# Weights transposed at the end of each slot and x1 added a slot earlier, in a cross-attention and FP4 feed-forward kernel

## What is computed

```python
def block(x, context, Wq, Wk, Wv, Wo, bo, w_gate, w_up, w_down):
    n = layernorm(x)
    q, k, v = n @ Wq, context @ Wk, context @ Wv          # 16 heads of 64
    attn = softmax(q k^T * 64**-0.5)                      # per head, 1024 x 154
    x = x + (attn v) @ Wo + bo                            # x1
    n = layernorm(x)
    gate, up = fp4(n) @ fp4(w_gate).T, fp4(n) @ fp4(w_up).T   # 704 hidden
    return x + fp4(silu(gate) * up) @ fp4(w_down).T
```

## Time and profile before

| | us |
|---|---|
| median of 3 runs | 984.53 (983.6 to 984.84) |
| the profiled execution, its own time | 986.75 |
| span of its trace, first to last instruction | 984.9 |
| PE busy | 857.0 (87%) |
| DVE busy | 757.5 (77%) |
| ACT busy | 534.0 (54%) |
| POOL busy | 529.5 (54%) |
| mean granted TensorE clock, share of full | 0.973 |

### The profile page before, as it was taken

One profiled execution on the slowest core, in us unless ns is written; L12 is line 12 of the kernel. 1 busy time (PEld: TensorE's weight loads), 2 busy tenths in 40 slices (PEclk: granted clock), 3 DMA queues, 4 the chain that ended last, 5 costly groups with the idle time before them and its releaser, 6 DMA issues.

```text
span 984.9 us, 21389 instructions
## 1 busy us (share of the span) xinstructions
PE 857.0 (87%) x6254; PEld 812.8 (83%) x6254; DVE 757.5 (77%) x2176; ACT 534.0 (54%) x1879; POOL 529.5 (54%) x677
## 2 busy tenths in 40 slices
PE   4786789999999999989989999989999999999874
PEld 3666789988888998888978888889888888888863
DVE  5857788877778888867878888876877888887762
ACT  4454455556565555556555555556555555655520
POOL 2545666554535656545554656554553656555651
PEclk9888999999999999999999999999999999999986
DMA  7101000001010000001000000001000000000000
GB/s 215 39 11 49 7 17 13 22 13 44 7 33 17 13 23 11 21 14 39 12 28 23 12 22 12 21 8 33 23 7 23 12 18 12 16 11 12 7 11 11
DMA packets 19869, 23.13 MB, mean 23 GB/s; under 512 B 2642, under 2 KB 18234, under 8 KB 19770
## 3 DMA queue, kind: packets, MB, share of 16 engines
q1 hardware_dynamic: 19770, 21.94, 7.2%
HBM read 17.74 MB, written 4.19 MB: 22 GB/s over the span
## 4 chain that ended last, share of the span: by engine, by line
PE 63%; DVE 21%; issue 8%; ACT 4%; POOL 2%; DMA 1%; DVEq 1%; SPq 0%; POOLq 0%; ACTq 0%
PE ps_g L1015 10%; PE ps_q L937 8%; PE ps_s L975 8%; PE ps_t L985 5%; PE ps_o L998 5%; PE ps_o L1000 5%; PE ps_o L999 5%; DVE negmax L782 3%; DVE pT_lo L637 3%; PE ps_m L865 3%; PE ps_g L900 3%; PE ps_m L1025 3%; PE ps_m L1027 2%; PE ps_m L1026 2%; DVE scales L667 2%
## 5 line engine op out<-in xcount | busy, mean ns | idle before, releaser
L472 POOL TENSOR_TENSOR probs<-probs,rsum 128x308 f32<-128x308 f32 x256 | 180.0, 703 | 284.2 <-DVE rsum L746 283.6
L610 ACT ACTIVATE probs<-ps_s,negmax 128x154 f32<-128x154 f32 x512 | 194.7, 386 | 229.4 <-DVE negmax L782 228.2
L998 PE MATMUL ps_o<-B_sb,pT_lo 128*128 128x256 f32 x640 | 183.6, 287 | 38.5 <-DVE x_both L804 33.9
L782 DVE TENSOR_REDUCE negmax<-ps_s 128x2 f32<-128x308 f32 x256 | 121.3, 474 | 78.4 <-PE ps_s L975 76.6
L1000 PE MATMUL ps_o<-B_sb,pT_hi 128*128 128x256 f32 x640 | 181.2, 283 | 0.0
L999 PE MATMUL ps_o<-B_sb,pT_hi 128*128 128x256 f32 x640 | 180.9, 283 | 0.0
L998 PEld LDWEIGHTS ps_o<-B_sb,pT_lo 128*128 128x128 f32 x640 | 121.7, 190 | 45.3 <-issue 42.9
L637 DVE TENSOR_TENSOR pT_lo<-ps_t,pT_hi 128x256 fp32r<-128x256 f32 (+1 forms) x256 | 122.7, 479 | 42.6 <-ACT pT_hi L514 37.4
L985 PE MATMUL ps_t<-ident,probs 128*128 128x128 f32 x640 | 115.0, 278 | 35.9 <-DVE pT_lo L637 35.3
L1015 PE MATMUL ps_g<-WGU,xqT_hi 128*128 128x352 f32 x512 | 136.6, 349 | 3.5 <-DVE B_sb L637 1.9
L514 ACT ACTIVATE pT_hi<-ps_t 128x256 fp32r<-128x256 f32 (+1 forms) x256 | 111.4, 435 | 29.1 <-PE ps_t L985 22.7
(11 more groups left out here) (149 smaller groups left out, 2236.7 us busy)
## 6 DMA issues: line engine op xcount, KB each, us to landing
xa<-in_x_dram SPq DMA_DIRECT2D x33, 128.0 KB, 2.1
xr<-in_x_dram SPq DMA_DIRECT2D x32, 128.0 KB, 2.0
out_dram<-y_xn SPq DMA_DIRECT2D x32, 128.0 KB, 1.7
W_sb<-in_L_xattn_Wk_dram SPq DMA_DIRECT2D x4, 512.0 KB, 4.4
W_sb<-in_L_xattn_Wv_dram SPq DMA_DIRECT2D x3, 512.0 KB, 3.6
probs<-in_L_xattn_Wq_dram SPq DMA_DIRECT2D x1, 1024.0 KB, 7.0
Wo_sb<-in_L_xattn_Wo_dram SPq DMA_DIRECT2D x1, 1024.0 KB, 6.6
VT<-in_ctx_dram SPq DMA_DIRECT2D x1, 384.0 KB
```

The lines of the kernel that those rows point to most:

```text
L472: pool.tensor_tensor(unit, unit, rsum[:, 2 * u:2 * u + 2].unsqueeze(2) .to_broadcast([P, 2, M]), ALU.mult).then_inc(norm_p, 1)
L610: ins = act.activation(probs[:, h, 0:M], ps_s[k % 2][:, s * M:(s + 1) * M], ACT.Exp, bias=negmax[:, h:h + 1], accum_out=sums[:, h:h + 1])
L782: dve.tensor_reduce(negmax[:, 2 * k:2 * k + 2], ps_s[k % 2][:, 0:UM].rearrange("p (h m) -> p h m", h=2), AX_X, ALU.max, negate=True).then_ ...
L998: pe.matmul(ps_o[:, 0:C], lo[:, j, :], w[:, 0:C], start=first, stop=False)
```

## The change

VectorE's add of the residual moves from the middle of its slot 4 to the end of its slot 3, with its waits. ScalarE's copy of x1 to `y`, which must come before it, moves from the end of slot 3 to the end of slot 2. On TensorE the transposes of the weights move from behind `attend` to behind all products of the slot (hidden and x transposes, gate and up, down, q, setup jobs); only the transposes of the raw weights of the start stay behind them.

```diff
@@ scalar: step
-                    if down and k == 3:
+                    if down and k == 2:
                         at = pair - 2 + par
                         act.wait_ge(x1_v, d + 1)
...
                         act.activation(y[1 - par], x1[1 - par], ACT.Copy).then_inc(y_a, 1)
@@ vector: step
                     if before and k == 4:
-                        dve.wait_ge(o_mm, PAIRS * (e + 1))
-                        dve.wait_ge(xr_p, e + 1)
-                        if some(d + 1):
-                            dve.wait_ge(y_a, d + 1)
-                        elif not some(e):
-                            dve.wait_ge(raw_mm, RAW_T[3])
-                        dve.tensor_tensor(x1[1 - par], xr[1 - par][:, :], ps_o[:, 0:C], ALU.add).then_inc(x1_v, 1)
                         if some(e):
                             dve.wait_ge(xln2_a, e)
                         stats(x1[1 - par], st2, mv2, ve2, nm2, (x1_v, e + 1), ln2_v, 5 * e)
...
+                    if before and k == 3:
+                        dve.wait_ge(o_mm, PAIRS * (e + 1))
+                        dve.wait_ge(xr_p, e + 1)
+                        if some(d + 1):
+                            dve.wait_ge(y_a, d + 1)
+                        elif not some(e):
+                            dve.wait_ge(raw_mm, RAW_T[3])
+                        dve.tensor_tensor(x1[1 - par], xr[1 - par][:, :], ps_o[:, 0:C], ALU.add).then_inc(x1_v, 1)
@@ tensor: step
                     if own and k >= 4:
                         attend(t, k - 4, setup if kind in ("start", "roll") else None)
-                    if before and k < 2:
-                        turn_probs(e, k + PAIRS - 2)
-                    if own and k >= 2:
-                        turn_probs(t, k - 2)
...
                     for job in jobs_at(setup, k):
                         make(job, setup[1])
+                    if before and k < 2:
+                        turn_probs(e, k + PAIRS - 2)
+                    if own and k >= 2:
+                        turn_probs(t, k - 2)
                     if turn_at(t, k, 0) is not None:
                         chunk_transposes(turn_at(t, k, 0))
```

## The result

The changed kernel takes 1008.46 us (median of 4 runs, 1006.26 to 1009.55) against 984.1 of the kernel before on the same chip: a ratio of 1.0244 (1.0225 to 1.0263). It is slower, as forecast, but by 24 us and not by 6, and half a microsecond past the upper end of the range.

The account below looks back on a forecast made before the run. No engine was taken to bound both halves of a tile pair alone: VectorE paced even slots 5 to 7, then TensorE. Terms of +6.9, +0.9, some -1 and a tail of nothing, about +6 on 984.5, gave 990 us, range 966 to 1,008.

Parts of the forecast that it names:

- The maximum of slot 5: VectorE, even tiles: starts 4.93 us after S, the start of slot 4's first score product, against 5.21 before.
- even to odd: From slot 4 of an even ordinary tile to slot 4 of the odd one: about +1.1 us, 27.2 against 26.07.
- odd to even: From slot 4 of an odd ordinary tile to slot 4 of the next even one: -0.2 us, 24.85 against 25.05.
- Tiles with setup jobs: Tiles v, k, roll and settle: TensorE paces them; their steps per eight tiles were -1.4, +1.1, -0.8 and +1.6 us.
- the start takes some 1 off: Start of the kernel: about 1 us gained, as what stands behind the waiting transposes waits for the same VectorE.
- into v: Step into the setup tile v: -1.4 us, saved at x1 and slot 7, less 0.7 in slots 1 and 2.
- v to k: Step from setup tile v to setup tile k: +1.1 us, reckoned as even to odd.
- k to roll: Step from setup tile k to roll: -0.8 us, x1's and slot 7's savings against later banks and a longer gate wait.
- roll to settle: Step from setup tile roll to settle: +1.6 us, x1 saves 1.54 but slots 6, 7 and 0 wait for VectorE.
- (A): Rival, whole kernel: faster, VectorE swallows the phase shift; 960 to 975 us, at best 951; chance 0.30.
- (C): Rival, nearly every slot: the hand-over stalls both engines, much slower, about 1,010 to 1,030 us; chance 0.12.
- (D): The forecast itself, whole kernel: slower by 0.2 to 2%, 986.5 to 1,003 us; chance 0.43.

Follow-up runs that it names:

- e10: Kernel before with the add of x1 in slot 3, and the transposes late only in tiles with setup jobs: 979.99 us.
- e6: Changed kernel with `xqT_hi` and `xqT_lo` of slot 2 ahead of the weights' parts on ScalarE and VectorE: 986.31 us.
- e1: Changed kernel with the transposes back at their old place behind the attention product, so only the add of x1 (and its copy) moved: 944.5 us.
- e11: Kernel before with the add of x1 in slot 3, and the transposes late only in tiles without setup jobs: 976.51 us.
- e7: Changed kernel with `xqT`, `hqT` and the maximum ahead of the weights' parts on ScalarE and VectorE: 964.82 us.
- e2: Kernel before with only the transposes moved to the end of the slot, the add of x1 still in slot 4: 1084.83 us.
- e8: Kernel before with the add of x1 in slot 3, and the transposes late only in slots 0 to 2: 979.43 us.
- e9: e1 with e7's order on ScalarE and VectorE, transposes at their old place: 1009.24 us.
- e5: e2 with VectorE's maximum ahead of `pT_lo`, `xqT_lo` and `hqT_lo`: 1071.86 us.

## Why the prediction was right in direction and too small

**In ordinary tiles the mechanism held.** The maximum of slot 5 comes at S+4.98 (4.93), even to odd takes 27.29 (27.2), odd to even 24.98 (24.85), so +1.15 a pair where +0.9 was forecast. A part of that gap is a slip in adding up: 0.04+0.49+0.67 is 1.20, which the sum carried as 1.1, and even to odd measured +1.21. The q product of slot 1 starts 4.19 us behind slot 0 of the odd tile (4.18 forecast). Its wait is shown as only 0.18 us, but it is counted from the end of the record before it (602.40), and records reach past the time in which the next can start. From the x transposes ahead of it to the q product it is 0.56 us (602.02 to 602.58) against 0.14 before (589.40 to 589.54), so 0.42 us are lost where 0.49 was forecast. The gate product starts at S+1.89 (605.53, with S at 603.64), 0.15 later than forecast; its wait is shown as 0.43 to 0.55 us in nearly all ordinary tiles. One wait was misread: the down product's for `xT_lo` is 1.3 us in the mean and 1.47 in this pair, not over 2, because the x transposes ahead of it, which waited for nothing there before, now wait 1.02 us at 592.07 for `hqT_lo`. The time of the step came out right all the same.

**What failed is the size of "Tiles with setup jobs" and "the start takes some 1 off".** The step that failed is "They have more TensorE work and TensorE paces them", by which most of the hand-over to VectorE was to be hidden there. The twelve setup steps were to cost 1.5 us in all and cost 13.0, and late transposes in setup tiles alone cost 35.5 (e10). The start with the first pair was to gain 0.1 and lost 4.2. The timeline of before and of after, first score product of slot 4 in the three settle tiles (318.05, 545.05, 770.33 and 324.80, 557.98, 792.12) and of the slot behind each turn of the outer loop:

```profile
318.05 0.30 PE L975 MATMUL ps_s<-K_hi,q_lo 128*128 128x308 f32 x1
...
436.83 0.52 PE L975 MATMUL ps_s<-K_hi,q_lo 128*128 128x308 f32 x1 [1.98 <-issue]
...
545.05 0.30 PE L975 MATMUL ps_s<-K_hi,q_lo 128*128 128x308 f32 x1
...
663.50 0.40 PE L975 MATMUL ps_s<-K_hi,q_lo 128*128 128x308 f32 x1 [1.65 <-issue]
...
770.33 0.30 PE L975 MATMUL ps_s<-K_hi,q_lo 128*128 128x308 f32 x1
```

```profile
324.80 0.39 PE L976 MATMUL ps_s<-K_hi,q_lo 128*128 128x308 f32 x1
...
445.24 0.40 PE L976 MATMUL ps_s<-K_hi,q_lo 128*128 128x308 f32 x1 [3.41 <-issue]
...
557.98 0.39 PE L976 MATMUL ps_s<-K_hi,q_lo 128*128 128x308 f32 x1
...
677.89 0.43 PE L976 MATMUL ps_s<-K_hi,q_lo 128*128 128x308 f32 x1 [2.92 <-issue]
...
751.68 0.58 PE L1016 MATMUL ps_g<-WGU,xqT_hi 128*128 128x352 f32 x2 [1.76 <-DVE B_sb L637]
...
792.12 0.39 PE L976 MATMUL ps_s<-K_hi,q_lo 128*128 128x308 f32 x1
```

The change loses 6.75 us up to the first of them, 6.18 and 8.86 in the two batches between, and 1.0 behind the last, together the 22.8 between the spans. (The forecast's terms add up to 6.8, which it rounded down to 6.) The terms of the prediction, each three times as in its sum, against the steps from slot 4 to slot 4 in the two traces:

| term | forecast, us | measured, us |
|---|---|---|
| start and first pair | -0.1 | +4.2 |
| into v, three | -4.2 | +1.2 (-0.88, +0.46, +1.60) |
| v to k, three | +3.3 | +4.0 |
| k to roll, three | -2.4 | +1.3 (-0.09, -0.11, +1.46) |
| roll to settle, three | +4.8 | +6.6 |
| ordinary, twelve steps | +5.4 | +6.9 |
| tail | 0 | -1.3 |
| sum | +6.8 | +22.8 |

Every term but the tail came out higher. The setup steps carry 11.6 us, the start 4.3 and the ordinary pairs 1.5; less the tail's 1.3 these are the 16 us that are missing. Of the 11.6, 2.7 are a longer idle at the turn of the loop and 3.0 a lower clock in the third batch, for which the prediction had no term. The other 5.9 are the steps themselves, each 0.2 to 0.7 us dearer than reckoned.

- *Into v.* 1.43 and 1.27 us of it are TensorE's longer "issue" idle (time in which it waited for nothing that the profile shows) at the turn of the outer loop (3.41 for 1.98, 2.92 for 1.65).
- *The clock.* In the third batch the longer idle is followed by a lower clock, as the windows behind it show, first of before and then of the changed kernel:

```profile
663.50:666.70 3.20, 3.20 (x24) 3.06 (x25) 2.49 (x7) 1.40 (x6) 1.79 (x3) 1.00 0.13 43
```

```profile
677.89:682.50 4.61, 4.61 (x24) 4.61 (x25) 2.13 (x6) 0.85 (x4) 2.09 (x3) 0.63 0.10 34
...
521.00:526.00 5.00, 5.00 (x37) 4.29 (x36) 2.31 (x8) 2.43 (x9) 3.31 (x5) 1.00 0.08 26
...
754.20:759.40 5.20, 5.20 (x30) 4.50 (x29) 2.22 (x7) 1.72 (x7) 2.76 (x5) 0.77 0.08 27
```

The same 24 products take 4.61 us instead of 3.20: 1.4 more. Behind the second loop turn before, with 1.65 us of idle, the clock stayed full. That the longer idle brought the lower clock is not shown: in e6 the idle was 2.91 us at both turns and the clock stayed at 1.00 behind each. Likewise the gate product of the roll tile waits 1.76 us for the bank of `B_sb` (751.68) against 0.64, the 1.0 longer that was forecast. In the first two roll tiles the clock stayed at 1.00 behind it (521 to 526 is the second) and slot 3 took 4.0 us; in the third the clock was 0.77 and slot 3 took 5.22. That is most of what sets the +1.46 in the table apart from the other two steps.
- *K to roll.* The first two steps, with a full clock, gave -0.1 and not -0.8. The terms that the prediction lists for it add up to -0.6, not -0.8.
- *Roll to settle and v to k* went as forecast within 0.6 us a step.
- *The start.* The 1 us that I took off is there: slot 4 of the first tile starts 0.99 us earlier. But from there to slot 4 of the second tile 2.9 us are lost, 1.7 of them in one slot, and 1.2 more by the third. The variants show what this goes with. At slot 4 of the second tile e1 is 3.4 us ahead of the kernel before, e11 (transposes late in ordinary tiles only) 2.8, and e7 (late everywhere, `pT_lo` last) 3.5, but e10 (late in setup tiles) is 1.1 behind and the changed kernel 1.9. So the start pays for late transposes with `pT_lo` first, as the other tiles do.

Why the idle at the turn of the loop is longer is not settled. In the kernels that have the transposes last in slot 7 of an ordinary tile, the last work of the loop's body, it was 2.4 to 3.6 us (the changed kernel, e2 to e7 and e11). In the others it was 1.7 to 2.1 (before, e1, e8, e9, e10). What makes it so is open.

**The rivals.** Of (A), the premise was true of one half of the change: without x1's wait TensorE keeps 39 us. I priced both moves as one and so handed the gain back in the same sentence. The rule that I argued against (the Trainium skill, "Perfetto Trace Analysis", "Optimization Strategy": remove what the busiest engine's gaps wait for) is borne out by e1, where removing 33.9 us of waits gave 39. The sum is larger than the waits mainly because each wait is shown 0.16 us shorter than what it costs (0.99 and 1.32 for 1.15 and 1.48), and because the same stand in the three roll tiles is put down to "issue" (4.6 us); the echo in slot 6 takes some 4 back. It is not borne out by the transposes: from e1 to the changed kernel their waits fell from 42.1 to 16.7 us, and the time rose by 64. (C), hand-over stalls in nearly every slot at 1,010 to 1,030, comes nearest in size; the result lies between it and (D)'s 1,003. But of the ordinary tiles' slots only 1, 2, 5 and the even 0 and 6 grew, slot 3 and the even 7 did not, and the odd 7 shrank by 0.9 us.

## What to carry to other kernels

Price each move of a compound change by itself, and then what each is worth when the other is in: here -39 and +101 made +24, and the better half alone beats both kernels (944.5 us). When a producer moves to the end of a slot, the consumers in order on other engines can hold up all that stands behind them. Here it paid neither to move the producer alone nor to move the consumers alone; with both moved most of the loss was gone, and leaving both was best. Ask for each new or longer wait of TensorE what the clock does behind it.

## What the runs showed of the hardware

- The granted clock fell after waits of under 2 us: after 1.94 us to 0.56 (e2), after 1.98 to 0.63 (before, 436.83 to 441.48), after 1.76 to 0.77 in one of three equal places. But it did not always fall: after 1.94 or 1.95 us it stayed at 1.00 in three tiles of e2, after 1.78 or 1.79 us it fell in 5 of 14 tiles of e5, and after 2.91 us at the loop's turn it stayed at 1.00 twice in e6. So the length of one wait doesn't decide it; each drop cost about 1.0 to 1.6 us. The Trainium skill, "TensorE: Matmul & The Clock Gate", "HAM oscillation — how this bites in real kernels", describes this loss for a kernel with longer stalls between bursts; these traces show it at stalls under 2 us.
- The scatter between runs goes in part with the clock. Of 19 runs of the kernel before on one chip, the fastest (978.52 us) had a mean of 0.983 and the slowest (987.92) one of 0.973: 9.4 us, where the clock alone would give 0.010 x 983 = 9.8. The runs between them follow it only loosely (985.07 us had 0.981).
